# Cross attention with top-32 selection: per-head steps replaced by a per-tile schedule, with heads summed on TensorE

## The reference

```
scores = q @ k.T / sqrt(32)          # per head, 2048 wide
kth    = 32nd largest score of the row
attn   = softmax(where(scores >= kth, scores, -inf))
ac     = mean over heads of attn @ ctx      # 4096 x 384
```

## Time and profile before

| what | us |
|---|---|
| median of 3 runs | 5832.1 |
| lowest and highest of them | 5827.6 and 5834.4 |
| span of the profiled execution | 5836.0 |
| VectorE busy over the span | 3252.9 |
| TensorE busy over the span | 3947.5 |
| ScalarE busy over the span | 1604.9 |
| GpSimd busy over the span | 2014.8 |

### The profile page before, as it was taken

The page is one execution under the profiler, slowest core; times in us unless marked ns, Lnnn a source line. Parts: engine busy times, 40 slices in busy tenths (PEclk is TensorE's granted clock), DMA queues, the critical chain, the costliest instruction groups (busy, mean ns, idle before and its releaser), DMA issues. The chain is left out here.

```text
span 5836.0 us, 62332 instructions
## 1 busy us (share of the span) xinstructions
PE 3947.5 (68%) x17990; PEld 3006.7 (52%) x18052; DVE 3252.9 (56%) x9545; ACT 1604.9 (27%) x2170; POOL 2014.8 (35%) x1374
## 2 busy tenths in 40 slices
PE   2422159996355455444545698796789999499998
PEld 1321037774233333233323486575668888388887
DVE  8959914442888888888888254552234343422222
ACT  1211013333555555444555100002221111111111
POOL 2447100000333433333433265140147676233332
PEclk8555569998666666666666799898889999799999
DMA  0025032225101001001100144223322121200000
GB/s 11 15 77 204 29 83 71 80 78 174 44 8 48 21 10 48 19 7 39 29 10 6 68 141 141 87 94 132 117 85 82 58 75 51 90 19 22 23 23 20
DMA packets 243466, 356.11 MB, mean 61 GB/s; under 512 B 67844, under 2 KB 121988, under 8 KB 238856
## 3 DMA queue, kind: packets, MB, share of 16 engines
q1 hardware_dynamic: 137728, 175.01, 10.1%
q10 hardware_dynamic: 102920, 169.93, 8.5%
q0 software_dynamic: 2560, 8.39, 0.4%
HBM read 246.29 MB, written 106.96 MB: 61 GB/s over the span
## 5 line engine op out<-in xcount | busy, mean ns | idle before, releaser
L2764 DVE CAST m_act_hl<-m_g 128x512 fp32r<-128x512 f32 x256 | 138.1, 539 | 894.9 <-ACT m_g L2652 894.9
L1381 POOL TENSOR_TENSOR xa_acc<-xa_acc,xa_prob 128x2048 f32<-128x2048 f32 x96 | 437.8, 4560 | 515.9 <-ACT xa_prob L1483 515.9
L2513 POOL TENSOR_TENSOR m_act_hl<-m_g,m_act_hl 128x512 fp32r<-128x512 f32 x256 | 353.3, 1380 | 702.6 <-DVE m_act_hl L2764 702.6
L1581 DVE MAX8 xa_cand<-xa_s_buf 128x8 f32<-128x64 f32 x4096 | 531.7, 210 | 52.2 <-issue 52.0
L2652 ACT ACTIVATE m_g<-m_ps_h,m_b 128x512 f32<-128x512 f32 x256 | 176.5, 689 | 1103.2 <-PE m_ps_h L82 1103.2
L1402 PE MATMUL xa_ps_f<-xa_ones,xa_flag 128*1 128x1 f32 x256 | 24.2, 164 | 629.5 <-DVEq L1597 629.3
L80 PE MATMUL m_ps_h<-m_hT,m_w 128*128 128x512 f32 x1024 | 412.7, 403 | 12.3 <-DVE m_w L2743 7.6
L1395 PE MATMUL xa_ps_s<-xa_ks,xa_qs 128*128 128x512 f32 x512 | 372.1, 810 | 70.4 <-ACT xa_s_buf L1476 36.4
L81 PE MATMUL m_ps_h<-m_hT,m_w 128*128 128x512 f32 x1024 | 404.8, 395 | 0.0
L82 PE MATMUL m_ps_h<-m_hT,m_w 128*128 128x512 f32 x1024 | 404.5, 395 | 0.0
L82 PE MATMUL m_ps_o<-m_w,m_act_hl 128*128 128x512 f32 x1024 | 404.3, 395 | 0.0
(11 more groups left out here) (374 smaller groups left out, 9957.3 us busy)
## 6 DMA issues: line engine op xcount, KB each, us to landing
at_xk<-in_x_dram SPq DMA_DIRECT2D x128, 128.0 KB, 2.7
xa_ks<-kt SPq DMA_DIRECT2D x64, 256.0 KB, 4.8
spectrum<-df_yo ACTq DMA_DIRECT2D x32, 512.0 KB, 2.8
id_raw<-spectrum SPq DMA_DIRECT2D x32, 512.0 KB, 3.8
m_xt<-x ACTq DMA_DIRECT2D x64, 256.0 KB, 3.3
bf_w_dn<-_L_ffn_down_weights_dram SPq DMA_DIRECT2D x7, 2048.0 KB, 7.2
bf_w_up<-in_L_ffn_up_weights_dram ACTq DMA_DIRECT2D x7, 2048.0 KB, 10.4
ky_raw<-in_ctx_dram SPq DMA_DIRECT2D x16, 768.0 KB, 6.6
```

What stands on the lines that cost most here:

```text
L1381: pool.tensor_tensor(acc[:, k, :], acc[:, k, :], prob[:, h % 2, :], ALU.add).then_inc(s_acc, 1)
L1581: dve.max(out=cand[:, 8 * g:8 * g + 8], in_=s_buf[:, slot, g * SEG:(g + 1) * SEG])
L2513: pool.tensor_tensor(lo, g32[:, :], hi.bitcast(F32), ALU.subtract).then_inc(s_gl, 1)
```

## The change

`stage_cross` is rewritten so that its unit is a tile of four heads.

- **Candidates.** The 8 largest of a segment are written rank by rank (`ranks`), 32 values apart. Ranks 1 to 3 of all segments (96 values) and the 8 largest of ranks 4 to 8 make 104 values, on which the four rounds run in place of 256. The count for doubt runs over two stretches of 104: it counts the eighth of those 8 twice, and the eighth of every segment.
- **Flags.** One flag column per head, one TensorE sum, one copy, one settle per tile, with four register loads and four branches.
- **Selecting.** The fused compare-and-multiply over 2048 stays on VectorE, and writes into `s_buf`.
- **Scaling, sum over heads and transpose.** ScalarE's multiplication by the reciprocal and GpSimd's three additions go. VectorE writes the reciprocals onto four 128 x 128 diagonals, and TensorE multiplies each 128-column block of each head's `s_buf` by them, adding the heads up in PSUM: 64 matmuls in plain fp32 per tile in place of 16 transposes.
- **Mask.** It becomes row 96 of the stacked keys, against ones in the queries, so the bf16 matmuls go. It is made once, in `stage_keys`, on VectorE from one partition of 8192, and stored to DRAM. GpSimd fills 32 partitions of `ks` and `qs` at the start of `stage_cross`, before any load.
- **Order.** All lists are written out over the 32 tiles, with no loops. SyncE issues the context loads and the stores that ScalarE issued. `s_buf` holds two tiles.

The diff, cut to its core (the definitions around it, semaphores and the removed lists are left out):

```
-def stage_keys(nc, A, kt_out):
+def stage_keys(nc, A, kt_out, km_out):
...
+                sp.dma_start(mask_u8[:, :], A["mask_BxS2_bf1"].rearrange("(o b) s -> o (b s)", o=1)).then_inc(s_ms, 16)
+                sp.wait_ge(s_mask, 1)
+                sp.dma_start(km_out.rearrange("(o b) s -> o (b s)", o=1), mask[:, :].bitcast(F32)).then_inc(s_mst, 16)
                 with sp.Fori(1, GROUPS // 2) as j:
...
+                dve.wait_ge(s_ms, 16)
+                dve.tensor_scalar(mask[:, :], mask_u8[:, :], BIG, -BIG, ALU.mult, ALU.add).then_inc(s_mask, 1)
...
-def stage_cross(nc, A, qt_in, kt_in, ac_out):
+def stage_cross(nc, A, qt_in, kt_in, km_in, ac_out):
...
-    NCAND = 8 * SEGS
+    KEEP = 3
+    NW = 8 + KEEP * SEGS
+    NC = 8 + 8 * SEGS
+    BACK = NC - NW
...
-        s_buf = sb("s_buf", [P, 4, S2])
+        s_buf = sb("s_buf", [P, 2, HEADS, S2])
-        acc = sb("acc", [P, 2, S2])
+        diag = sb("diag", [P, HEADS, P])
...
+                    sp.dma_start(ks[96:97, h, :].bitcast(F32), km_in[b:b + 1, :]).then_inc(s_ks[h], 16)
...
+                sp.wait_ge(s_const, 3)
+                queries(0)
...
+                pool.memset(ks[96:128, :, :].bitcast(F32), 0.0)
+                pool.memset(qs[96:128, :, :, :].bitcast(F32), 1.0)
+                pool.drain().then_inc(s_const, 1)
...
-                            pool.tensor_tensor(acc[:, k, :], acc[:, k, :], prob[:, h % 2, :], ALU.add).then_inc(s_acc, 1)
...
                     for c in range(4):
-                        pe.matmul(ps_s[:, c, :], qs[:, k, h, :], ks[:, h, c * 512:(c + 1) * 512], start=True, stop=False)
-                        last = pe.matmul(ps_s[:, c, :], row0[:, :], mask[:, c * 512:(c + 1) * 512], start=False, stop=True)
+                        last = pe.matmul(ps_s[:, c, :], qs[:, t % 2, h, :], ks[:, h, c * 512:(c + 1) * 512], start=True, stop=True)
...
-                        last = pe.transpose(ps_t[:, g % 2, q, :], acc[:, k, c * P:(c + 1) * P], ident[:, :])
+                    for c in range(8):
+                        k0 = half * HALF + c * P
+                        last = pe.matmul(ps_t[:, c // 4, c % 4, :], s_buf[:, t % 2, h, k0:k0 + P], diag[:, h, :],
+                                         start=(h == 0 and c % 4 == 0), stop=(h == HEADS - 1), skip_group_check=True)
+                    last.then_inc(s_dg, 1)
...
+                for t in range(TILES):
+                    sum_flags(t)
+                    if t >= 1:
+                        mix(t - 1)
+                    if t + 1 < TILES:
+                        scores(t + 1, 2)
+                    turn(t, 0, 0)
+                    turn(t, 0, 1)
+                    if t + 1 < TILES:
+                        scores(t + 1, 3)
+                    turn(t, 0, 2)
+                    turn(t, 0, 3)
+                    turn(t, 1, 0)
+                    if t + 2 < TILES:
+                        scores(t + 2, 0)
+                    turn(t, 1, 1)
+                    turn(t, 1, 2)
+                    turn(t, 1, 3)
+                    if t + 2 < TILES:
+                        scores(t + 2, 1)
...
-                    act.activation(acc[:, k, :] if h == 0 else prob[:, h % 2, :], prob[:, h % 2, :], ACT.Identity,
-                                   scale=rec[:, h % 2, :]).then_inc(s_scl, 1)
...
+                    if t + 1 < TILES:
+                        copy(t + 1, 1)
+                    denominators(t)
+                    exponentials(t, 0)
+                    exponentials(t, 1)
+                    if t + 1 < TILES:
+                        copy(t + 1, 2)
+                    exponentials(t, 2)
+                    if t + 1 < TILES:
+                        copy(t + 1, 3)
+                    exponentials(t, 3)
...
+                    hi(t, 0)
+                    hi(t, 1)
+                    if t + 2 < TILES:
+                        copy(t + 2, 0)
...
+                    hi(t, 2)
+                    hi(t, 3)
...
+                ranks = cand[:, 8:NC].rearrange("p (r g) -> p r g", g=SEGS)
+                def scan(t, h, first, last):
+                    if first == 0:
+                        dve.wait_ge(s_sc, HEADS * t + h + 1)
+                    for g in range(first, last):
+                        dve.max(out=ranks[:, :, g], in_=s_buf[:, t % 2, h, g * SEG:(g + 1) * SEG])
+                def rank(t, h):
+                    k = t % 2
+                    dve.drain()
+                    dve.max(out=cand[:, 0:8], in_=cand[:, NW:NC])
+                    dve.drain()
+                    src = cand[:, 0:NW]
...
+                def select(t, h):
+                    dve.wait_ge(s_exp, HEADS * t + h + 1)
+                    dve.scalar_tensor_tensor(out=s_buf[:, t % 2, h, :], in0=s_buf[:, t % 2, h, :],
+                                             scalar=top[:, t % 2, h, TOPK - 1:TOPK], in1=prob[:, h % 2, :],
+                                             op0=ALU.is_ge, op1=ALU.mult).then_inc(s_sel, 1)
...
+                    for h in range(HEADS):
+                        dve.tensor_scalar(diag[:, h, :], ident[:, :], rec[:, h:h + 1], None, ALU.mult)
+                    dve.drain().then_inc(s_diag, 1)
+                for t in range(-1, TILES):
+                    more = t + 1 < TILES
+                    if more:
+                        scan(t + 1, 0, 0, 8)
+                    if t >= 0:
+                        dve.wait_ge(s_f, t + 1)
+                        dve.tensor_copy(flag_i[:, :], ps_f[:, :])
+                        dve.drain()
+                    if more:
+                        scan(t + 1, 0, 8, 16)
+                    if t >= 0:
+                        settle(t)
+                    if more:
+                        scan(t + 1, 0, 16, SEGS)
+                        rank(t + 1, 0)
+                    if t >= 0:
+                        diagonals(t)
+                        select(t, 0)
+                        select(t, 1)
+                    if more:
+                        scan(t + 1, 1, 0, SEGS)
+                        rank(t + 1, 1)
+                    if t >= 0:
+                        select(t, 2)
+                        select(t, 3)
+                    if more:
+                        for h in range(2, HEADS):
+                            scan(t + 1, h, 0, SEGS)
+                            rank(t + 1, h)
+                        dve.tensor_scalar(nmax[:, (t + 1) % 2, :], top[:, (t + 1) % 2, :, 0], -SCALE, None, ALU.mult)
+                        dve.drain().then_inc(s_cand, 1)
```

More of the change, by code:

```diff
@@ L1292, in stage_cross @@
         s_st = [sem(f"mix_stored{k}") for k in range(2)]
[L1294 to L1309, removed]
         with nc.Block() as block:
@@ new lines, in _ @@
+                context(0, 0)
+                context(0, 1)
+                for t in range(TILES):
+                    b = t // TPB
+                    if t + 2 < TILES:
+                        queries(t + 2)
+                    if t % TPB == TPB - 2 and b + 1 < B:
+                        for h in range(HEADS):
+                            keys(b + 1, h)
+                        context(b + 1, 0)
+                        context(b + 1, 1)
+                    if t % TPB == 0:
+                        context(b, 2)
+                        context(b, 3)
+                    if t >= 1:
+                        store(t - 1)
@@ L1397, in scores @@
                     last.then_inc(s_s, 1)
-                def sum_flag(n, k):
-                    pe.wait_ge(s_cand, n + 1)
-                    pe.matmul(ps_f[:, k:k + 1], flag[:, k, :], ones[:, :], start=True, stop=True).then_inc(s_f, 1)
-                def turn(t, k, g):
-                    if g == 0:
-                        pe.wait_ge(s_acc, 3 * (t + 1))
-                    pe.wait_ge(s_a32, t * 4 + g - 1 if g >= 1 else t * 4)
-                    for q in range(4):
-                        c = 4 * g + q
-                        last = pe.transpose(ps_t[:, g % 2, q, :], acc[:, k, c * P:(c + 1) * P], ident[:, :])
-                    last.then_inc(s_aT, 1)
@@ L1414, in mix, with sum_flags, turn @@
-                def mix(t, b):
-                    pe.wait_ge(s_aTl, t * 4 + 4)
-                    pe.wait_ge(s_clo, 4 * (b + 1))
-                    pe.wait_ge(s_acc_c, t)
+                def sum_flags(t):
+                    pe.wait_ge(s_cand, t + 1)
+                    if t >= 1:
+                        pe.wait_ge(s_chk, t)
+                    pe.matmul(ps_f[:, :], ones[:, :], flag[:, t % 2, :], start=True, stop=True).then_inc(s_f, 1)
+                def turn(t, half, h):
+                    if half == 0:
+                        pe.wait_ge(s_sel, HEADS * t + h + 1)
+                    if h == 0:
+                        pe.wait_ge(s_diag, t + 1)
+                        if 4 * t + 2 * half >= 1:
+                            pe.wait_ge(s_a32, 4 * t + 2 * half)
+                    for c in range(8):
[3 more added lines that the diff above has]
+                    last.then_inc(s_dg, 1)
@@ L1450, in _ @@
```

(22 more changed lines are left out.)

405 lines of the change are left out of this document (155 added, 250 removed).

## The result

The kernel after takes 5630.7 us (median of four runs, 5620.3 to 5640.6) against 5833.2 beside it: a ratio of 0.9655 [0.9641, 0.9669], 202.5 us less. The profiled execution spans 5638.9 us against 5836.0, so 197.1 less.

A forecast was written before the change was run, and what follows sets the result against it. VectorE's own list was taken as the bound: tiles of 46.0 us plus 0.8 wait, with fill, doubts and collisions, made the stage 1593.6, 168.6 less; plus 10.5 for starts gave 5678 profiled, 5674 median, range 5605 to 5840.

The forecast's parts named there:

- one sign of being wrong: Prediction wrong if VectorE waits for exponentials at all, over 2 us a tile for the flag sum, or over 1 elsewhere.
- Settle: VectorE's register loads and branches on the four flags: 4.3 us a tile, between 1.26 and 5.0.
- Wait for the flag sum: VectorE waits for TensorE's flag sum, its first turns slow and the rest fast: 0.8 us put on each tile.
- Select: VectorE's fused select without the drain and the wait on the flag: 2.4 us each, 9.6 a tile.
- Scan, rank and count: VectorE's list per tile: scan unchanged at 16.9 us, narrower rank 11.6, count for doubt 2.2.
- GpSimd's collisions: Cross attention: GpSimd's context split can meet a select once a batch, 4 x 4 us, plus 10 for small splits: 26.
- Starts: Starts of keys and cross stages wait for mask and fills: 6 and 4.5 us, 10.5 together, between nothing and 16.
- Doubts: Cross attention: the same three doubts are settled, at 23.0 us each, 69 us in all.
- TensorE at 1.2 GHz as the bound: Slow turns ahead of the flag sum make tiles 56 us, 285 more in all, 5959; chance 0.09.
- Waits at several places: VectorE waits on ScalarE or TensorE, four us a tile, as for head 3's late exponentials: 5798; chance 0.14.
- The strided store: MAX8's stores 128 bytes apart cost: 0.078 us on each of 128 x 32, 320 us, 5994; chance 0.03.
- Every skip stalls: Each skip of a settle on VectorE stalls like the loop's return, 4.05 us: 518 in all, 6192; chance 0.02.

The follow-up runs named there:

- experiment 4: Kernel after with one register load and one branch a tile, behind a maximum over the four flags, in place of four each: 5568.4 us, 62.3 less.
- Experiment 3: Kernel after with 28 unused plain fp32 matmuls a tile added on TensorE, ahead of the last scores and the flag sum: 5785.3 us, 154.6 more.
- experiment 6: Kernel before with the compute engines' loops over batches and pairs of cross attention written out: 5808.6 us, 20.7 less.

## Why the prediction was right, and by how much it was off

The forecast case came: VectorE's list sets the tile, TensorE stays behind it, no wait of weight shows but in the settle, and the doubts are three. By the letter one sign of being wrong was met, a wait for exponentials: 0.8 us in the whole stage, in the last tile. The 35.4 us by which the stage beat its forecast come from terms of the sum, not from the mechanism.

- **Settle: 3.0 against 4.3.** The cast takes 0.23 and the pause 2.77. I took 1.26 as mostly load and branch and multiplied it. By the two pauses of 1.12 (one pair) and 2.77 (four), a further pair costs 0.55; by experiment 4, 0.78. Either way a part of the 1.12 does not repeat.
- **Wait for the flag sum: 0.03 a tile against 0.8.** In the tile shown the sum starts at 2062.22 and the copy reads it at 2063.28. I had TensorE's last scores ready at 48 into the tile; they end at 2061.70, 44.3 in. Head 3's select ended at 29.1, not 30.4, and the chain behind it took 15.2 us where I had 17.6: only the first nine or so of the sixteen matmuls behind the pause, of heads 2 and 3, ran slow (32 records in 5.88 us, where 48 took 5.52). Where the turn behind ScalarE's copies is slow as well, the chain is 1.5 us longer.
- **Select: 9.1 against 9.6.** Without the step's drain and flag wait two in a row take 4.53 (2029.68 to 2034.21).
- **Scan, rank and count: 31.3 against 30.7.** Rank with count is 3.50 a head, forecast 3.45; head 0's scan, cut in three, takes 4.56 where the others take 4.23, 0.2 of it for the late flag sum. The four MAX8 of 160 took 0.33 each, forecast 0.4. **Diagonals and maximum: 1.55 against 1.4.** Sum: 44.9. The prediction's 43.0 to 46.8 for the tile takes in the ends of the settle alone; with those of the diagonals its own figures give 42.4 to 47.0.
- **GpSimd's collisions: 51.8 against 26.** I priced the context's split against one select a batch, 16 us. That was near: four selects lost 12.7. But the split also meets line 1639 and the count, and the four tiles in which it falls lose 30.8. The subtraction of line 1367 (1276 ns) costs 0.5 to 1.9 us in 19 of the other 27 tiles, 21.1 in all where I had 10. Line 1639 has four values a row and little work; its place made it dear. The collisions gave back 26 us of the 66 that the tile saved (31 x 2.13, by the 44.67), and the short pauses 7 more.
- **Starts: 6.8 against 10.5.** The first scan is that much later. But the keys stage itself begins 2.0 us earlier in this profile (1360.4 against 1362.3), and from 1355.9 to 1362.3 over all profiles, with the stages ahead of it unchanged. From its first instruction to the first scan it is 108.6 us against 99.8: the two starts cost 8.8, and the 2.0 lie in that scatter. Mask and fills show as 4.42 us on VectorE (one partition of 8192) and 6.92 + 0.95 on GpSimd. Which part was covered was not tried by itself. **Tail: 35.7, forecast the same as 35.2.**
- **Doubts: three, 68.0 against 69.** The stage makes 35.4 of the 43.3 us by which the point was missed, the starts 3.7; the rest is mostly that the median stands 8.2 below the profiled span, where I took 3.9.
- **TensorE's price per matmul:** 48 records in 5.52 us, 0.23 a matmul, forecast 0.24 at 2.4 GHz; 16 records in 3.51 us, 0.44, forecast 0.42 at 1.2 GHz. The clock granted over the stage is 0.82, between the levels of 1.2 and 2.4 GHz and well over 0.64, as the prediction's last part asked.

The rivals. *TensorE at 1.2 GHz as the bound* had its place right and was nearer than its 0.09 looks. Experiment 3 shows that work in front of the flag sum costs nearly its full length in two tiles of three. In the tile shown the turns were back at the upper level before the second half (16 records in 2.02 us), and 1.4 us more on that chain would have passed unseen; in ten tiles TensorE reached the sum without a pause. *Waits at several places*: did not come. *The strided store*: 32 MAX8 that write 128 bytes apart take 4.15 us, from start to start 4.22 to 4.23 where they took 4.23, so the price is nothing; the cacheline rule that the prediction cites from the Trainium skill (SBUF — State Buffer, the box on cachelines) does not show in these rows. *Every skip stalls*: four skips with their loads took 2.77 together. A forward jump over the settling of a doubt costs no such pause as the loop's return (5.17, and 20.7 us of time by experiment 6).

How the 202 us split over the parts is not the sum of single edits. Taken alone, the short rank gives 74.6 (83.5 when taken out of after), the thin additions 46.1, the written-out loops 20.7: 141 together. The rest, some 60 us, is not shown by an experiment; what is left for it are the settle and the steps merged to one a tile, the select without its drain, and what the parts give each other.

## What to carry to other kernels

Price a short instruction by where it falls, not only by its size: look at what GpSimd runs at that moment, and move the little ones to an engine that does not stand for it, as ScalarE here. When one engine's list sets the time, a helper engine is free for whatever fits into its long pause, and can cost its whole length once it stands in front of the one value that is waited for. Register loads and branches are part of the list: fold several tests into one.

## What the runs showed of the hardware

- A VectorE multiply of 128 x 4 values took 169 ns alone and up to 3219 ns beside a GpSimd subtraction; the fused count took 433 to 2650 ns in after, and its 25 long ones all overlap a GpSimd subtraction (line 1568, median 434). MAX8 of 64 never took more than 241 ns in 4096 (line 1550).
- A register load with its branch cost VectorE 0.78 us beyond the first in experiment 4 (2.77 against 0.43 for three fewer), and 0.55 by the 1.12 of before; four forward skips with their loads took 2.77 us, one step with a loop's return 5.17.
- The same 28 matmuls a tile cost nothing that can be measured, or 155 us, by their place in TensorE's list.
- The same turn of 16 records behind the same idle of 2.25 us took 2.02 us in one tile and 3.51 in another, by the level of TensorE's clock; the granted clock over the stage was 0.82.
